# Sixteen-head global attention on one core: from one head at a time to four heads in 32-row groups, with key-major scores

## The reference

```python
HEADS = 16
HEAD_DIM = HIDDEN // HEADS
SCALE = HEAD_DIM ** (-0.5)
q = (hidden_states @ Wq.T + bq).reshape(b, s, HEADS, HEAD_DIM)
...
scores = jnp.einsum('bqhd,bkhd->bhqk', q, k)
probs = jax.nn.softmax(scores.astype(jnp.float32), axis=-1).astype(scores.dtype)
out = jnp.einsum('bhqk,bkhd->bqhd', probs, v).reshape(b, s, d)
return out @ Wo.T + bo
```

## Time and profile before

| | us |
|---|---|
| median of 3 runs | 6022.95 (6012.32 to 6030.93) |
| the profiled execution | 6025.09 |
| its span, first to last instruction | 6023.3 |
| PE busy in it | 5290.3 |
| mean granted TensorE clock | 0.953 of full speed |

### The profile page before, as it was taken

How to read it: one execution, slowest core, us unless ns; L and a number is a source line. 1 busy time by engine, 2 the same in 40 slices (tenths; PEclk the granted TensorE clock), 3 DMA queues, 4 the chain that set the end, 5 groups by cost and what they waited for, 6 DMA issues and landing times. The chain is left out here.

```text
span 6023.3 us, 112187 instructions
## 1 busy us (share of the span) xinstructions
PE 5290.3 (88%) x34984; PEld 3858.1 (64%) x34984; DVE 4948.4 (82%) x8818; ACT 4123.4 (68%) x12293; POOL 3433.0 (57%) x2277
## 2 busy tenths in 40 slices
PE   7999899999999999999999999999999997576666
PEld 6999666666666666666666666666666665333333
DVE  4666688889888898888888898888888885778877
ACT  3555477777777777777777777777777775555443
POOL 1222366666666666666666666666666662434444
PEclk9999899999999999999999999999999998788787
DMA  1000000000000000000000000000000000000000
GB/s 20 4 3 3 23 1 0 0 0 10 10 0 0 0 12 8 0 0 5 14 1 0 0 6 14 1 0 0 9 5 0 0 0 4 1 2 2 3 3 4
DMA packets 35423, 25.54 MB, mean 4 GB/s; under 512 B 11316, under 2 KB 29303, under 8 KB 35191
## 3 DMA queue, kind: packets, MB, share of 16 engines
q1 hardware_dynamic: 26302, 22.22, 1.2%
q10 hardware_dynamic: 8888, 0.45, 0.1%
HBM read 20.57 MB, written 2.10 MB: 4 GB/s over the span
## 5 line engine op out<-in xcount | busy, mean ns | idle before, releaser
L1145 POOL TENSOR_TENSOR b_w<-b_w,b_vt 128x512 f32<-128x512 f32 x768 | 980.8, 1277 | 1412.7 <-DVE b_vt L1054 778.9
L1149 POOL TENSOR_TENSOR b_rn<-b_ssm,all_neg_half 128x16 f32<-128x16 f32 x384 | 1126.8, 2934 | 32.0
L971 ACT ACTIVATE b_PT<-ps 128x512 f32<-128x512 f32 x768 | 461.2, 601 | 458.3 <-PE ps L826 457.6
L953 ACT ACTIVATE b_Pr<-ps,b_nm 128x128 f32<-128x128 f32 x1536 | 564.9, 368 | 287.5 <-DVE b_nm L1086 285.0
L1086 DVE TENSOR_REDUCE b_nm<-ps 128x4 f32<-128x640 f32 x768 | 630.8, 821 | 125.2 <-PE ps L806 113.5
L872 PE MATMUL ps<-b_Whi,b_xlo 128*128 128x512 f32 x1152 | 596.3, 518 | 91.2 <-DVE b_vt L1054 78.1
L955 ACT ACTIVATE b_Pr<-ps,b_nm 128x160 f32<-128x160 f32 x1536 | 611.2, 398 | 0.0
L1052 DVE TENSOR_TENSOR b_w<-ps,until_b_rotab 128x512 f32<-128x512 f32 x768 | 529.3, 689 | 26.4 <-ACT b_sq L986 6.1
L986 ACT ACTIVATE b_sq<-ps 128x512 f32<-128x512 f32 x768 | 468.0, 609 | 81.4 <-PE ps L874 80.9
L1054 DVE TENSOR_TENSOR b_vt<-ps,until_b_rotab 128x512 f32<-128x512 f32 x768 | 523.2, 681 | 0.0
L1056 DVE TENSOR_REDUCE b_ss<-b_sq 128x8 f32<-128x512 f32 x768 | 519.7, 677 | 0.0
(11 more groups left out here) (256 smaller groups left out, 13935.0 us busy)
## 6 DMA issues: line engine op xcount, KB each, us to landing
b_Wraw<-in_L_ffn_Wqkv SPq DMA_DIRECT2D x36, 256.0 KB, 2.9
b_Wo<-in_L_ffn_Wo SPq DMA_DIRECT2D x6, 512.0 KB, 4.1
a_xtok<-in_L_attn_hidden_states SPq DMA_DIRECT2D x16, 128.0 KB, 2.1
out<-c_xout SPq DMA_DIRECT2D x16, 128.0 KB, 1.8
b_W<-in_L_ffn_W SPq DMA_DIRECT2D x6, 341.0 KB, 2.9
setup_wmod<-in_L_wmod SPq DMA_DIRECT2D x2, 384.0 KB
b_W<-in_L_ffn_W SPq DMA_DIRECT2D x6, 128.0 KB
setup_rot<-in_rot SPq DMA_DIRECT2D x1, 256.0 KB
```

The costliest lines, as they stand in the source:

```text
L953: nc.scalar.activation(s.Pr[:, p % 2, j, 0:P], ps[:, S_BANK[j], WIN:KEYS], ACT.Exp, bias=s.nm[:, h, 0:1], accum_out=s.ssum[:, h, 0:1])
L1145: nc.gpsimd.tensor_tensor(rows, rows, s.vt[:, i % 4], ALU.add).then_inc(s.pool_add, 1)
L1149: nc.gpsimd.tensor_tensor(s.rn[:, j], s.ssm[:, j], g.neg_half[:, 0:HB], ALU.pow).then_inc(s.pool_r, 1)
```

## The change

A step of `phase_a` has 4 places (`at`) instead of 16 slots, each for 4 heads. The columns of the weights are spread so that head j of the four has its 8 features at the start of a group of 32 partitions, the other 24 being zero; q and k are therefore projected four times per sequence (`project`). Per four heads, PE makes query-major scores for the maximum alone, two heads at a time (`scores`); DVE takes the negated maxima of two heads with one instruction; PE turns them into rows, which ACT copies; PE makes the scores a second time with keys on the partitions, and adds the negated maxima with a second product (`ones_rows` times `nmT`) into the same bank; ACT takes four exponentials of 512 columns, which are the turned probabilities already. PE multiplies them with v, whose heads lie 32 columns apart with a column of ones for the sum, the outputs of four heads going to four groups of 32 partitions; ACT copies, PE turns back, DVE divides. `qm` on POOL, the transposes of the probabilities and their copies are gone. The two layer norms of the stage are applied by ACT instead of DVE, with a shift that POOL multiplies out. The first norm is a step earlier, the residual and the second norm a step later. One bank, A, serves the turned maxima, the turned outputs, v, the output projection and the residual's transposes; another, B, serves q and k, the product with v, and the norms' transposes. The diff, cut to what the prediction speaks of:

```diff
-        small += [(g.bqk[:, 0:1], flat(d["L0_attn_bq"])), (g.bqk[:, 1:2], flat(d["L0_attn_bk"])), (g.head_rows[:], d["head_rows"])]
+        for at, name in enumerate(("L0_attn_bq", "L0_attn_bk")):
+            for j in range(4):
+                small.append((g.bqk4[32 * j:32 * j + D0, at], d[name].rearrange("(i r) -> r i", i=4)[D0 * j:D0 * (j + 1)]))
...
+            nc.gpsimd.memset(g.bqk4[:], 0.0)
+            nc.gpsimd.memset(g.wq4[:], 0.0)
+            nc.gpsimd.memset(g.wk4[:], 0.0).then_inc(s.consts, 1)
...
-T_LAG, PV_LAG = 2, 3
...
+GROUP, QUADS = 4, H0 // 4
...
-        s.qm = s.sb("qm", [P, 2, H0, NT])
...
+        s.q4 = s.sb("q4", [P, 2, QUADS, NT]); s.k4 = s.sb("k4", [P, 2, QUADS, NT])
+        s.V = s.sb("V", [P, 2, TT, H0, HROWS]); s.ones_rows = s.sb("ones_rows", [P, P])
+        s.nmz = s.sb("nmz", [P, 2, TT, GROUP, HROWS]); s.nmT = s.sb("nmT", [P, NT])
+        s.PT = s.sb("PT", [P, GROUP, TT, NT]); s.OT = s.sb("OT", [P, NT])
...
-        S_BANK, T_BANK, O_BANK, FRONT_BANK, TAIL_BANK = (0, 1), (2, 3), (4, 5), 6, 7
...
+        S_BANK, ST_BANK, A_BANK, B_BANK = (0, 1), (2, 3, 4, 5), 6, 7
...
+        def quad(step, at, lag):
+
+            if at >= lag:
+                return (step.n, at - lag, step.odd) if step.heads else (None, None, None)
+            return (step.n - 1, at - lag + QUADS, 1 - step.odd) if step.tail else (None, None, None)
...
+            nc.vector.memset(s.nmz[:], 0.0)
+            nc.vector.memset(s.ones_rows[:], 0.0)
+            nc.vector.memset(s.V[:], 0.0).then_inc(s.prepared, 1)
...
+                    for pair in range(2):
+                        if step.heads:
+                            i = 2 * at + pair
+                            dve.wait_ge(s.s_done, 2 * QUADS * n + i + 1)
+                            nc.vector.tensor_reduce(s.nmz[:, at % 2, :, 2 * pair:2 * pair + 2, 0].rearrange("p t j -> p j t"),
+                                                    ps[:, S_BANK[0]:S_BANK[1] + 1].rearrange("p j (t k) -> p j t k", t=TT),
+                                                    AX.X, ALU.max, negate=True).then_inc(s.max_done, 1)
+                        if pair == 0:
+                            if step.last and at == 1:
+                                dve.wait_ge(s.x2_full, u + 1)
+                                nc.vector.tensor_copy(s.x2tok[:], ps[:, A_BANK, 0:NT].rearrange("p (t e) -> p t e", t=TT)).then_inc(s.x2tok_ready, 1)
...
+                            if step.front and at == 2:
+                                dve.wait_ge(s.v_full, f + 1)
+                                nc.vector.tensor_copy(s.V[:, pf, :, :, 0:D0], ps[:, A_BANK, 0:NT].rearrange("p (t h e) -> p t h e", t=TT, e=D0)).then_inc(s.v_ready, 1)
...
+                        dve.wait_ge(s.o_full, QUADS * item + i + 1)
+                        both = ps[:, A_BANK, 0:NT].rearrange("p (t g r) -> p t g r", t=TT, g=GROUP)
+                        nc.vector.reciprocal(s.rinv[:], both[:, :, :, D0]).then_inc(s.recip, 1)
...
-                        nc.gpsimd.tensor_tensor(s.qm[:, pf, some], s.qT[:].rearrange("p (o t) -> p o t", o=1).broadcast_to((P, heads, NT)),
...
+                def store_qk(i):
+
+                    act.wait_ge(s.qk_full, QUADS * f + i + 1)
+                    nc.scalar.activation(s.q4[:, pf, i], ps[:, B_BANK, 0:NT], ACT.Identity, bias=g.bqk4[:, 0, i:i + 1], scale=float(D0) ** -0.5)
+                    nc.scalar.activation(s.k4[:, pf, i], ps[:, B_BANK, NT:2 * NT], ACT.Identity, bias=g.bqk4[:, 1, i:i + 1]).then_inc(s.qk_ready, 1)
+
+                for at in range(QUADS):
+                    item, i, parity = quad(step, at, 1)
+                    if item is not None:
+                        act.wait_ge(s.nm_full, QUADS * item + i + 1)
+                        nc.scalar.activation(s.nmT[:], ps[:, A_BANK, 0:NT], ACT.Copy).then_inc(s.nm_ready, 1)
+                    item, i, parity = quad(step, at, 2)
+                    if item is not None:
+                        act.wait_ge(s.pv_done, QUADS * item + i + 1)
+                        nc.scalar.activation(s.OT[:], ps[:, B_BANK, 0:NT], ACT.Copy).then_inc(s.ot_ready, 1)
+                    if step.front and at == 0:
...
+                    if step.front and at >= 1:
+                        store_qk(at - 1)
...
+                    item, i, parity = quad(step, at, 1)
+                    if item is not None:
+                        act.wait_ge(s.st_done, QUADS * item + i + 1)
+                        for j in range(GROUP):
+                            last = nc.scalar.activation(s.PT[:, j], ps[:, ST_BANK[j]].rearrange("p (k t) -> p k t", k=TT), ACT.Exp)
+                        last.then_inc(s.exp_done, 1)
+                    if step.front and at == 3:
+                        store_qk(3)
...
-                        wait(act, s.qm_ready, QM_PIECES * f)
-                        nc.scalar.activation(s.qT[:], ps[:, FRONT_BANK, 0:NT], ACT.Identity, bias=g.bqk[:, 0:1], scale=float(D0) ** -0.5)
-                        nc.scalar.activation(s.kT[:, pf], ps[:, FRONT_BANK, NT:2 * NT], ACT.Identity, bias=g.bqk[:, 1:2]).then_inc(s.qk_ready, 1)
+                        nc.scalar.activation(s.oT[:], ps[:, A_BANK, 0:NT], ACT.Copy).then_inc(s.oT_ready, 1)
...
+                def scores(i, pair):
+
+                    wait(pe, s.max_done, 2 * QUADS * n + 2 * i + pair)
+                    for tt in range(TT):
+                        for j in range(2):
+                            r = rows_of(2 * pair + j)
+                            last = nc.tensor.matmul(ps[:, S_BANK[j], tt * NT:(tt + 1) * NT], s.q4[r, pa, i, tt * P:(tt + 1) * P], s.k4[r, pa, i],
+                                                    start=True, stop=True, skip_group_check=True)
+                    last.then_inc(s.s_done, 1)
...
+                def project(i):
+
+                    nc.tensor.matmul(ps[:, B_BANK, 0:NT], g.wq4[:, i].rearrange("p g r -> p (g r)"), s.hT[:], start=True, stop=True)
+                    nc.tensor.matmul(ps[:, B_BANK, NT:2 * NT], g.wk4[:, i].rearrange("p g r -> p (g r)"), s.hT[:], start=True, stop=True).then_inc(s.qk_full, 1)
+
+                for at in range(QUADS):
...
+                        if at == 0:
+                            pe.wait_ge(s.qk_ready, QUADS * n + QUADS)
+                        scores(at, 0)
+                    item, i, parity = quad(step, at, 1)
+                    if item is not None:
+                        pe.wait_ge(s.max_done, 2 * (QUADS * item + i) + 2)
+                        if at == 0 and step.last:
+                            pe.wait_ge(s.tmp_ready, u + 1)
+                        elif at == 1 and step.last:
+                            pe.wait_ge(s.x2tok_ready, u + 1)
+                        elif at == 2 and step.front:
+                            pe.wait_ge(s.v_ready, f + 1)
+                        elif at == 3 and step.tail:
+                            pe.wait_ge(s.oT_ready, t + 1)
...
+                            last = nc.tensor.transpose(ps[:, A_BANK, tt * P:(tt + 1) * P], s.nmz[:, i % 2, tt].rearrange("p g r -> p (g r)"), g.ident[:])
+                        last.then_inc(s.nm_full, 1)
+                    item, i, parity = quad(step, at, 2)
+                    if item is not None:
+                        pe.wait_ge(s.exp_done, QUADS * item + i + 1)
...
                         for kb in range(TT):
+                            for j in range(GROUP):
+                                last = nc.tensor.matmul(ps[rows_of(j), B_BANK, 0:NT], s.V[:, parity, kb, GROUP * i + j], s.PT[:, j, kb],
+                                                        start=kb == 0, stop=kb == TT - 1, skip_group_check=True)
+                        last.then_inc(s.pv_done, 1)
+                    if step.heads:
+                        scores(at, 1)
+                    item, i, parity = quad(step, at, 2)
+                    if item is not None:
+                        pe.wait_ge(s.ot_ready, QUADS * item + i + 1)
...
+                        for tt in range(TT):
+                            last = nc.tensor.transpose(ps[:, A_BANK, tt * P:(tt + 1) * P], s.OT[:, tt * P:(tt + 1) * P], g.ident[:])
+                        last.then_inc(s.o_full, 1)
+                    if step.front:
...
+                        else:
+                            if at == 1:
+                                pe.wait_ge(s.hT_ready, f + 1)
+                            if at > 1:
+                                pe.wait_ge(s.qk_ready, QUADS * f + at - 1)
+                            project(at - 1)
+                    if step.last and at == 2:
...
+                            pe.wait_ge(s.qk_ready, QUADS * f + 2)
...
+                    item, i, parity = quad(step, at, 1)
+                    if item is not None:
+                        pe.wait_ge(s.nm_ready, QUADS * item + i + 1)
+                        wait(pe, s.exp_done, QUADS * item + i)
+                        for kb in range(TT):
+                            for j in range(GROUP):
```

(56 more changed lines are left out.)

309 lines of the change are left out of this document (130 added, 179 removed).

## The result

The changed kernel takes 6141.93 us, median of 4 runs (6124.79 to 6159.50), against 6019.05 (6012.32 to 6030.93) of the kernel before, run beside it: ratio 1.0191, 95% interval 1.0163 to 1.0219. It is slower by about 123 us. The profiled execution has a span of 6157.7 us, 134.4 more than that of before.

What follows compares the result with a forecast made beforehand. PE was taken to bound the first stage. Chain -17, ends +3 and clock +22 summed to +8 on the execution's 6025.1, 6033; the median lies 2.1 below, so 6030 us, no change; range 5950 to 6150.

Steps and rivals of the forecast that it cites:

- the rival on the clock: First stage: granted clock falls as in the third stage or deeper, mean 0.75, +137 us, 6150; chance 0.09.
- the signs that the prediction named for being wrong: First stage in the new profile: a clock of 1.00 and a period under 36, or passes starting one after another.
- Overlap and change of form: PE, first stage: four groups overlap fully; a change of form costs about 0.20 us; 32 key-major passes take 1.73.
- The rivals of pairs: PE's four groups overlap only in pairs: +2.6 us per four heads, +166, 6190; chance 0.14, partly for a loss in between.
- no overlap: PE's passes each run alone: about +550 us, 6580; chance 0.04.
- The chain and its waits: First stage, per sequence: 30.1 us chain, lengthened by bank A and queue waits to 38.1 against 39.18; gain 17 us in 16.
- The ends: Setup, fill and last chain of the first stage: together +3 us, setup +3.3 of it; first scores near 61 us.
- The clock: First stage's granted clock taken as 0.95: 1.35 us a sequence, +22 us.
- The first rival: First stage: clock holds and waits are shorter; 6009 without the clock's part, 5932 if bank A waits hide, 5985 middle; chance 0.34.
- Without the clock's part: The sum leaving out the clock's price: 6023 - 14 = 6009 us.

Runs made afterwards that it cites:

- e1_fill: The changed kernel with 12 unread matmuls per sequence on PE, placed just ahead of waits it has anyway: 5977.9 us, ratio 0.9913.
- e7_before_idle: The kernel before, with PE waiting for an unread POOL operation in four slots of each sequence: 6405.7 us, ratio 1.0626.
- e5_fill_two: The changed kernel with unread matmuls, 4 and 3 per sequence, ahead of only the two waits for DVE's copies: 6005.5 us, ratio 0.9958.
- e2_dve: The changed kernel with DVE's copies of v and the residual's turn ahead of the pair-0 maximum instead of behind it: 5969.7 us, ratio 0.9905.

## Why the prediction was right or wrong

The forecast of 6030, no change, was wrong; the range held the time; it came out as the rival on the clock that had 0.09 (mean 0.75, 6150; measured 0.76 and 6142). That this rival's time is so near is partly luck: its price for the clock was 137 us, and the first stage shows 163, while the code behind that stage happened to take 10 us less than before, and the median lies 18 us below the profiled execution. A low clock with a longer period was not among the signs that the prediction named for being wrong.

- **Overlap and change of form: right.** Key-major scores and subtraction were 0.20 + 1.73; measured 1.94. The rivals of pairs and of no overlap are out. The Trainium skill's 3.07 times for four row groups, "TensorE: Matmul & The Clock Gate", Part 3, is given there for 512 columns and is not what this trace shows with 256: 0.216 us for four passes, what one takes alone, a full fourfold; the measurement decides.
- **The chain and its waits: right.** 38.1 us a sequence at full clock against 37.40 in e1_fill. The waits stand where they were put: v, the residual's turn, the output turn, the second norm's turn and the next sequence's scores are the first five rows of the waits. The maximum over 1024 columns took 1226 ns for 1.21.
- **The ends: nearly right.** The first scores came at 63.13 for 61; the setup's first work on ACT began 3.8 us later, where I had 3.3.
- **The clock: this step failed.** "I take 0.95, 25.6 x (1/0.95 - 1) = 1.35 a sequence, +22 us". Measured: 0.74, and 49.5 - 37.4 = 12.1 us a sequence; 164 us between the changed kernel and e1_fill. Two errors lie in it. I judged the gaps one at a time, by their length ("its gaps are as short as in the second"), and so put the stage near the second; e1_fill and e7_before_idle show that waits of about 1 to 2 us, none longer than 2.2, lower it to 0.74 when enough of them recur through a sequence. The first rival's ground, that PE's longest gap is under what the earlier trace rows shows, didn't fit the prediction's own figure either: 2.0 of 3.40 us stood empty there, and it had put up to 2.8. And the formula is too mild: at 0.74 it gives 9.0 us a sequence for the 12.1 measured. It spreads the mean clock evenly, while the low stretches are those where PE is nearly always busy. The six low stretches between the stores of v at 216.99 and 315.94 hold 50.8 us of busy PE, 25.4 a sequence, and half of that is 12.7, near what was measured.
- **Without the clock's part: right.** My sum gave 6009, 14 less than before; e1_fill shows 5978, but only 18.8 us of its gain lie ahead of the second stage. So at full clock the change is a gain of some 19 us, with twelve matmuls a sequence more, and the clock that its own waits bring down takes back 163 (and not 16 times 12.1, since the first and last sequences lose less).

The Trainium skill tells of such a thing in "TensorE: Matmul & The Clock Gate", section "A second HAM failure mode: psum-queue depth-cycling": PE that idles for short times between groups of matmuls, as PSUM banks are handed round, lets the clock swing between its levels. The trace agrees: 1.00 and 0.50 in turn, with bank A behind three of the six waits. It need not be a bank: the waits of e7_before_idle are for POOL, and its clock is 0.74 as well.

## What to carry to other kernels

When a change shortens PE's work, add up the short waits that it leaves, and don't look at the longest alone: the clock may take back more than the waits cost (14.8 us against 9.2 in e7_before_idle). Whether a given set of them is harmless has to be measured, as e5_fill_two shows. Price a low stretch at about half the time that PE is busy in it (3.2 us for 6.80 in e2_dve). To tell waits from clock, fill the waits with matmuls that nobody reads; and where a bank is handed over, put the copy that frees it ahead of long work in its engine's queue, which was worth 172 us here.

## What was not expected of the hardware

More work on PE made the kernel faster by 164 us, on an unchanged chain. One kernel ran in two regimes within one execution: e2_dve at 34.54 us a sequence up to 290 us and mostly at 37.7 behind it, e5_fill_two at 40.7 and later 37.5. And four row groups of 32 rows overlap without any loss that the trace shows.
